# A GRU with a ternary FFN behind it: the FFN starts two groups behind the GRU, the first eight steps have two PSUM banks per sum, and the weight quantisation is spread over twelve steps

## The chip, the cores and the metric

One Trainium2 chip, one core of it. The metric is the device time of one execution in microseconds; lower is better. Before the change the median of 3 runs is 365.18 us (363.53 to 365.69).

## What is computed

A GRU runs over 32 time steps for 128 sequences of width 256, from a given first state. Every state then goes through an FFN whose weights are made ternary in groups of 64, and the result is added to the input. Biases of the GRU are not zero. All is float32 except the quantisation, which is bfloat16.

```python
def cell(h, x):
    gi = x @ W_ih + b_ih
    gh = h @ W_hh + b_hh
    r = sigmoid(i_r + h_r); z = sigmoid(i_z + h_z)
    n = tanh(i_n + r * h_n)
    h_new = (1.0 - z) * n + z * h

w = w_fp32.astype(bfloat16); w_g = w.reshape(-1, 64)
scale = clip(mean(abs(w_g)), 1e-08, None)
q = clip(round(w_g / scale), -1, 1)
w_hat = q * scale                      # used as w + (w_hat - w)

gu = x @ wq_gu.T                       # 256 -> 2 * 1024
h = silu(gate) * up
hn = h * rsqrt(mean(h * h) + eps)
return hn @ wq_p.T                     # 1024 -> 256
```

## The kernel before

One engine program each for SyncE (loads and stores), GpSimd (POOL), ScalarE (ACT), VectorE (DVE) and TensorE (PE), tied by semaphores. The order on every engine is written out by hand.

**The GRU step** (t = 0 to 31). Every float32 product is split in three passes of a rounded form: high parts of data and weights, high data by low weights, low data by high weights. PE's state product adds to the bank ps_rz (r and z, 512 columns, so one sigmoid serves both) and to the second half of ps_n (256 columns). ACT takes the sigmoid (L294). DVE makes r_hn and n_pre (L434, L436) and zh (L437), ACT the tanh (L307), DVE zm_n and the new state h_nat (L443, L446). PE transposes h_nat (L639), ACT rounds it to the high part (L311), DVE makes the low part (L450). With the high part the next state product can start. Between the sigmoid and the transposes PE adds the product of the next input to ps_rz, behind the transposes that to ps_n. Both banks are single: before the next input's product ACT copies the bias into them (seed_rz after the sigmoid, L299; seed_n after n_pre, L303). The split of the input is done by ACT (L314) and by DVE (L455), in steps 2 to 5 by GpSimd (L252).

**The FFN** works on groups of four steps, 512 columns, one group behind the GRU. Per group there are eight tiles j: gate product G and up product U (four matmuls of 512 columns each, L646), sigmoid on ACT (silu_part, L318), gated and hidden on DVE (L460, L470: gsg, then hid), hid_hi and the square on ACT (L322, L332), hid_lo and the sum of squares on GpSimd (L258, L265), and the down product D (eight matmuls of 256 columns, L685) into ps_out. C6 and C7 are the down products of tiles 6 and 7 of the group before, S its sums of squares by token. rows_out (L484) scales ps_out, adds the input from x_all and writes o_st, which SyncE stores. The items are placed among the steps by the tables PE_BEFORE and PE_AFTER (ahead of and behind the transposes; "in" and "n" are the next input's products). U of tile j waits for hid of tile j-1, since ps_up is one bank. A group's states must lie together, so at each fourth step ACT and DVE copy three states into grp_hi and grp_lo. After step 31 the last group runs alone by PE_ALONE.

**The quantisation** has six units of 1024 columns: four of the gate and up weights, two of the down weights. Per unit: Abs (L338) and Sign (L343) on ACT, group sums on PE (L724, two matmuls), means on ACT (L353), seven operations on DVE (two of scales L493, L494; ternary L502, L504; L509; L511; signed L516) and the rounded weight on ACT (L347). One unit is done per step, steps 0 to 5; in steps 4 and 5 beside the first FFN group. Raw weights lie in x_all, which is loaded with the input only when the last sign is done.

**Start.** Two bias rows come by DMA, three products with a row of ones spread them over the partitions (plain float32), four small matmuls follow (keep_clock), and the input product waits for the split of the input weights, the state product for that of the state weights. Groups 2 to 6 are in a hardware loop on each engine, groups 0, 1 and 7 are written out.

## Time and profile before

| what | value |
|---|---|
| median of 3 runs | 365.18 us (363.53 to 365.69) |
| profiled execution, its own time | 364.85 us |
| its span in the trace | 363.0 us |
| PE busy | 345.6 us, 95% of the span |
| DVE, ACT, POOL busy | 234.0 (64%), 225.6 (62%), 164.5 (45%) us |
| chain that ended last, PE's share | 81% |
| mean granted TensorE clock | 0.986 |
| load of x_all, 4 MB, from issue to landing | 13.5 us |

The span runs from the first to the last recorded instruction; the time is 1.85 us more. A page row gives an engine's busy time in tenths for 40 equal slices. PE is the matmul stream, PEld the weight loads beside it. A matmul's own duration has a tail that overlaps the next one, so on a full PE durations add up to more than the time. A timeline row has the start, the duration, engine, line, operation, output from input, shapes, count, and in brackets how long the engine sat idle before it and for whom.

### The profile page before, as it was taken

To read this page: it belongs to the slowest core of one execution; us is meant where nothing else is said; L and a number is where in the kernel's file an instruction comes from. 1 tells how busy PE (TensorE), PEld (TensorE's weight loads), DVE (VectorE), ACT (ScalarE), POOL (GpSimd) and SP (SyncE) were. 2 spreads that over 40 slices of the span, in tenths; PEclk is the share of its full clock that TensorE was granted. 3 is DMA by queue.
4 is the path that set the end of the run, shared out by engine and by line. 5 is a ranking of instruction groups with operands and counts; after the bars stand their busy time and mean duration, and the time that the engine had idled before them with its cause. 6 is when DMAs were issued, how large, how long until landed. Compare 5 with 4: busy or idle time off the path is not lost.

```text
span 363.0 us, 5759 instructions
## 1 busy us (share of the span) xinstructions
PE 345.6 (95%) x1959; PEld 296.8 (82%) x1962; DVE 234.0 (64%) x446; ACT 225.6 (62%) x422; POOL 164.5 (45%) x141
## 2 busy tenths in 40 slices
PE   6978888799999999999999999999999999999995
PEld 4756666688888898888888898888888898888884
DVE  3698998845865567555865567555865567456643
ACT  5898996557366566657366566657366566546650
POOL 1111014336455363446455363446455363448881
PEclk9989999899999999999999999999999999999997
DMA  7990019000000001000000001000000001000101
GB/s 238 378 397 0 2 47 413 4 2 0 28 32 0 3 1 58 0 0 0 31 27 0 0 0 58 0 0 0 32 26 0 0 0 60 0 1 2 58 2 58
DMA packets 5394, 17.75 MB, mean 49 GB/s; under 512 B 386, under 2 KB 2050, under 8 KB 4996
## 3 DMA queue, kind: packets, MB, share of 16 engines
q1 hardware_dynamic: 5380, 17.57, 12.5%
q8 instruction: 8, 0.13, 0.2%
q14 instruction: 6, 0.05, 0.0%
HBM read 13.38 MB, written 4.19 MB: 48 GB/s over the span
## 4 chain that ended last, share of the span: by engine, by line
PE 81%; DVE 9%; ACT 4%; issue 3%; DMA 1%; SPq 0%; POOL 0%; POOLq 0%; DVEq 0%
PE ps_out L685 16%; PE ps_gate L646 15%; PE ps_up L646 14%; PE ps_rz L627 4%; PE ps_rz L603 4%; PE ps_n L603 4%; PE ps_rz L628 4%; PE ps_rz L604 4%; PE ps_rz L631 4%; PE ps_n L604 3%; PE ps_n L606 3%; PE ps_rz L606 3%; PE ps_hT L639 2%; DVE o_st L509 2%; PE ps_gate L696 1%
## 5 line engine op out<-in xcount | busy, mean ns | idle before, releaser
L258 POOL TENSOR_TENSOR hid_lo<-work,hid_hi 128x512 fp32r<-128x512 f32 x63 | 82.3, 1307 | 145.5 <-ACT hid_hi L322 145.5
L460 DVE TENSOR_TENSOR work<-work,ps_gate 128x512 f32<-128x512 f32 x64 | 43.9, 685 | 44.2 <-ACT work L318 43.4
L265 POOL TENSOR_TENSOR sq_sum<-sq_sum,work 128x512 f32<-128x512 f32 x54 | 71.4, 1322 | 0.0
L646 PE MATMUL ps_gate<-grp_hi,wguT 128*128 128x512 f32 x128 | 50.9, 398 | 0.0
L646 PE MATMUL ps_up<-grp_hi,wguT 128*128 128x512 f32 x118 | 47.2, 400 | 3.3 <-DVE work L470 3.3
L646 PE MATMUL ps_gate<-grp_lo,wguT 128*128 128x512 f32 x128 | 50.3, 393 | 0.0
L294 ACT ACTIVATE rz<-ps_rz 128x512 f32<-128x512 f32 x32 | 19.0, 595 | 47.3 <-PE ps_rz L631 46.9
L322 ACT CAST hid_hi<-work 128x512 fp32r<-128x512 f32 x63 | 38.7, 615 | 14.2 <-DVE work L470 14.2
L646 PE MATMUL ps_up<-grp_lo,wguT 128*128 128x512 f32 x118 | 46.6, 395 | 0.0
L470 DVE TENSOR_TENSOR work<-work,ps_up 128x512 f32<-128x512 f32 x59 | 40.5, 687 | 8.3 <-PE ps_up L646 6.8
L318 ACT ACTIVATE work<-ps_gate 128x512 f32<-128x512 f32 x64 | 37.8, 590 | 11.3 <-PE ps_gate L646 11.2
L434 DVE TENSOR_TENSOR r_hn<-rz,ps_n 128x256 f32<-128x256 f32 x32 | 13.5, 420 | 48.4 <-PE ps_n L606 48.4
L685 PEld LDWEIGHTS ps_out<-wpT,hid_hi 128*128 128x128 f32 x256 | 38.1, 189 | 4.4 <-DVE o_st L484 0.5
L685 PE MATMUL ps_out<-wpT,hid_hi 128*128 128x256 f32 x256 | 41.2, 283 | 0.1
L685 PE MATMUL ps_out<-wpT,hid_lo 128*128 128x256 f32 x256 | 41.0, 282 | 0.0
L685 PEld LDWEIGHTS ps_out<-wpT,hid_lo 128*128 128x128 f32 x256 | 35.1, 189 | 0.0
L332 ACT ACTIVATE work<-work 128x512 f32<-128x512 f32 x55 | 34.6, 629 | 0.0
L646 PEld LDWEIGHTS ps_up<-grp_hi,wguT 128*128 128x128 f32 x118 | 22.2, 188 | 8.8 <-DVE work L470 4.5
L311 ACT CAST new_hi<-ps_hT 128x256 fp32r<-128x256 f32 x24 | 8.9, 373 | 30.4 <-PE ps_hT L639 30.3
L603 PE MATMUL ps_rz<-wi_hi,xT_hi 128*128 128x512 f32 x64 | 26.6, 416 | 1.1 <-ACT ps_rz L299 0.7
L646 PEld LDWEIGHTS ps_gate<-grp_hi,wguT 128*128 128x128 f32 x128 | 24.1, 188 | 3.6 <-issue 0.2
L646 PEld LDWEIGHTS ps_gate<-grp_lo,wguT 128*128 128x128 f32 x128 | 24.1, 188 | 3.3
(116 smaller groups left out, 713.3 us busy)
## 6 DMA issues: line engine op xcount, KB each, us to landing
x_all<-in_x_dram SPq DMA_DIRECT2D x1, 4096.0 KB, 13.5
out_dram<-o_st SPq DMA_DIRECT2D x7, 512.0 KB, 2.6
xT_all<-in_x_dram SPq DMA_DIRECT2D x1, 3072.0 KB, 19.5
x_all<-in_L_ffn_w_gate_up_dram SPq DMA_DIRECT2D x4, 512.0 KB, 9.3
x_all<-in_L_ffn_w_proj_dram SPq DMA_DIRECT2D x1, 1024.0 KB, 12.8
work<-in_L_cond_W_ih_dram SPq DMA_DIRECT2D x2, 384.0 KB, 4.0
work<-in_L_cond_W_hh_dram SPq DMA_DIRECT2D x2, 384.0 KB, 5.8
xT_all<-in_x_dram SPq DMA_DIRECT2D x1, 768.0 KB, 8.0
```

The costliest lines, as they stand in the source:

```text
L258: nc.gpsimd.tensor_tensor(hid_lo[:, j % RING], hid[:, j % 2], f32(hid_hi[:, j % RING]), ALU.subtract).then_inc(hid_lo_ok, 1)
L265: nc.gpsimd.tensor_tensor(sq_sum[:], sq_sum[:], hid_sq[:, j % 2], ALU.add).then_inc(sq_added, 1)
L318: nc.scalar.activation(sg[:, j % 2], ps_gate[:, j % 2], ACT.Sigmoid).then_inc(sg_ok, 1)
L322: nc.scalar.copy(hid_hi[:, j % RING], hid[:, j % 2]).then_inc(hid_hi_ok, 1)
L332: nc.scalar.activation(hid_sq[:, j % 2], hid[:, j % 2], ACT.Square).then_inc(hid_sq_ok, 1)
L460: nc.vector.tensor_tensor(gsg[:, j % 2], sg[:, j % 2], ps_gate[:, j % 2], ALU.mult).then_inc(gsg_ok, 1)
L470: nc.vector.tensor_tensor(hid[:, j % 2], gsg[:, j % 2], up_bank(G, j)[:], ALU.mult).then_inc(hid_ok, 1)
L603: pe.matmul(dst, hi[:, k, :], w_hi[:, k, cols], start=False, stop=False, skip_group_check=True)
L604: pe.matmul(dst, hi[:, k, :], w_lo[:, k, cols], start=False, stop=False, skip_group_check=True)
L606: mm = pe.matmul(dst, lo[:, k, :], w_hi[:, k, cols], start=False, stop=stop and k == KD - 1, skip_group_check=True)
L646: mm = pe.matmul(bank, w, part[:, k].rearrange("p s b -> p (s b)"), start=(k == 0 and i == 0), stop=(k == KD - 1 and i == 1))
L685: mm = pe.matmul(ps_out[:, s, :], part[:, j % RING, s * P:(s + 1) * P], wpT[:, j, :], start=(j == 0 and s % 2 == 0 and part is hid_hi), st ...
```

## The change

- The FFN starts behind step 7, not step 3. Steps 0 to 7 run alone, steps 8 to 31 carry groups 0 to 5 by the same tables (PE_FIRST takes the place of the last column for group 0, with D4 and D5 behind the transposes), and groups 6 and 7 run alone at the end, by PE_ALONE each (PE_END closes).
- In steps 0 to 7 each sum has two banks, ps_rz and ps_up, ps_n and a half of ps_gate, and PE itself adds the bias: the bias is split in a high and a low row with changed sign (b_split), multiplied by two rows of -1. ACT's bias copies start with step 8.
- The quantisation takes two steps per unit in steps 0 to 7 (units 0 to 3), and units 4 and 5 stand in pieces in steps 8 to 11. Units are in the order in which the FFN wants them, and the down weights load as two.
- States stay in rings of 12 (st_hi, st_lo); grp and its copies are gone. The input for the last addition lies in a ring of 24 rows, the last 8 are loaded after the second store.
- GpSimd splits the inputs of steps 2 to 9. PE begins with 12 and later 6 matmuls on zeros. No hardware loop is left, all groups are written out.

```diff
 QG = 64
 EPS = 2.0 ** -23
 RING = 4
+LEAD = 8
+SR = 12
+XR = 24
 
 
 PE_BEFORE = [["C6", "G0", "in", "C7", "S"], ["G2", "U2", "in", "D0"],
              ["G4", "U4", "in", "D2"], ["G6", "U6", "in", "G7", "D4", "U7"]]
 PE_AFTER = [["U0", "n", "G1", "U1"], ["n", "G3", "U3", "D1"], ["n", "G5", "U5", "D3"], ["n", "D5"]]
...
+PE_FIRST = [["G6", "U6", "in", "G7", "U7"], ["n", "D4", "D5"]]
...
+        def rz_bank(t):
+            return ps_up if early(t) and t % 2 else ps_rz
+
+        def n_bank(t):
+            return ps_gate[:, 0, :] if early(t) and t % 2 else ps_n[:]
+
...
-            free = isinstance(G, int) and (G == NG - 1 and j % 2 or G == NG - 2 and j == HT - 1)
+            free = G >= NG - 2 and j % 2 or G == NG - 3 and j == HT - 1
             return ps_rz if free else ps_up
...
+        def state(parts, t):
+            return parts[:, :, t % SR, :]
+
+        def group_state(parts, G, k):
+            first = GS * G % SR
+            return parts[:, k, first:first + GS, :].rearrange("p s b -> p (s b)")
+
+
+        units = [("gu", 0), ("gu", HT), ("pj", 0), ("gu", 4), ("gu", HT + 4), ("pj", 4)]
...
+            for u in range(1, NU):
+                load_unit(u)
+            sp.wait_ge(b_split_ok, 1)
+            sp.dma_start(xT_all[:, :, LEAD:T, :], xt[:, :, LEAD:T, :]).then_inc(ld_xr, 16)
             sp.wait_ge(q_sign_ok, NU)
-            sp.dma_start(x_all[:], x).then_inc(ld_x, 16)
...
+            sp.dma_start(x_ring[:], x[:, 0:XR, :]).then_inc(ld_x, 16)
...
+                if G == (T - XR) // GS - 1:
+                    sp.dma_start(x_ring[:, 0:T - XR, :], x[:, XR:T, :]).then_inc(ld_x, 16)
...
+            for t in range(2, LEAD + 2):
+                pool.wait_ge(x_hi, t + 1)
+                nc.gpsimd.tensor_tensor(xT_lo[:, t % 2], xT_all[:, :, t, :], f32(xT_hi[:, t % 2]),
                                         ALU.subtract).then_inc(x_lo_early, 1)
...
+            for t in range(LEAD):
+                u, odd = divmod(t, 2)
+                rz_gates(t)
+                if odd:
+                    q_signs(u)
+                elif u:
+                    q_means(u)
+                n_gate(t)
+                if odd:
+                    q_abs_of(u + 1)
+                elif u:
+                    q_weights(u - 1)
+                else:
+                    q_means(0)
+                state_hi(t)
+                if t == 0:
+                    act.wait_ge(ld_x1, 16)
+                if t == LEAD - 2:
+                    act.wait_ge(ld_xr, 16)
+                input_hi(t + 2)
...
+                if t == LEAD:
+                    q_means(4)
+                if t == LEAD + 1:
+                    q_means(5)
+                n_gate(t)
+                if t < T - 1:
+                    seed_n(t + 1)
+                if t == LEAD:
+                    q_weights(3)
+                if t == LEAD + 1:
+                    q_signs(4)
+                if s == 3:
+                    silu_part(G, 6)
+                if s:
+                    hidden_parts(G, 2 * s - 1)
+                silu_part(G, 7 if s == 3 else 2 * s)
+                state_hi(t)
+                if t == LEAD + 3:
+                    q_weights(5)
+                hidden_parts(G, 2 * s)
+                if s < 3:
+                    silu_part(G, 2 * s + 1)
+                if t == LEAD:
+                    q_abs_of(5)
+                if t == LEAD + 1:
+                    q_weights(4)
+                if t == LEAD + 2:
+                    q_signs(5)
...
+            nc.vector.memset(q_keep[:], 0.0).then_inc(warm_ok, 1)
...
+            nc.vector.tensor_tensor(b_all[:, RZ], b_all[:, RZ], b_rows[:, 0:2 * D], ALU.add).then_inc(b_sum_ok, 1)
+            dve.wait_ge(b_sum_ok, 1)
+            nc.vector.tensor_copy(b_hi, b_all).then_inc(b_hi_ok, 1)
...
+            nc.vector.scalar_tensor_tensor(out=b_split[:], in0=f32(b_hi), scalar=ident[0:2, 1:2], in1=b_all,
+                                           op0=ALU.mult, op1=ALU.subtract).then_inc(b_split_ok, 1)
...
+                u, odd = divmod(t, 2)
+                candidate(t)
+                new_state(t)
+                if odd:
+                    difference(u)
+                else:
+                    scales(u)
+                state_lo(t)
+                if odd:
+                    magnitude(u)
+                    signed(u)
+                else:
+                    ternary(u)
+
...
+                if t == LEAD + 1:
+                    difference(4)
+                    magnitude(4)
+                if t == LEAD + 2:
+                    ternary(5)
+                if t == LEAD + 3:
+                    magnitude(5)
+                    signed(5)
+                gated(G, 2 * s)
+                if s:
...
+                    ternary(4)
+                if t == LEAD + 1:
+                    signed(4)
+                    scales(5)
+                if t == LEAD + 2:
+                    difference(5)
+                if G and s == 0:
+                    rows_out(G - 1)
+
+            for G in (NG - 2, NG - 1):
...
+                return pe.matmul(dst, neg_ones[:], b_split[:, cols], start=start, stop=False, skip_group_check=True)
+
+            def seed_rz(t):
+                bias_rows(rz_bank(t)[:], RZ, True)
+
+            def seed_n(t):
+                bias_rows(n_bank(t)[:, 0:D], N_IN, True)
+                bias_rows(n_bank(t)[:, D:2 * D], N_HID, False)
+
+            def input_rz(t):
+                if t > LEAD:
+                    pe.wait_ge(rz_seed, t - LEAD)
+                if t < 2:
...
+                    pe.wait_ge(q_w_ok, 1 if j == 0 else 4)
+                if j == 1 and 0 < G < NG - 2:
...
+
+            pe.wait_ge(warm_ok, 1)
+            busy(12)
+            pe.wait_ge(consts, 5)
+            pe.wait_ge(b_split_ok, 1)
+            bias_rows(ps_gate[:, 1, :], RZ, True)
+            bias_rows(q_sums[:, 0, 0:D], N_IN, True)
+            bias_rows(q_sums[:, 0, D:2 * D], N_HID, False).then_inc(biased, 1)
+            seed_rz(0)
+            seed_n(0)
+            busy(6)
             pe.wait_ge(wi_ok, KD)
...
+                state_product(t)
+                seed_rz(t + 1)
+                input_rz(t + 1)
+                seed_n(t + 1)
+                if t == 0:
+                    pe.wait_ge(bias_ok, 2)
+                    q_group_sums(0)
+                transpose_state(t)
+                input_n(t + 1)
+                if t % 2:
+                    q_group_sums((t + 1) // 2)
+
+            for t in range(LEAD, T):
+                g, s = divmod(t, GS)
+                G = g - LEAD // GS
+                before, after = PE_BEFORE[s], PE_AFTER[s]
+                if s == 3 and G == 0:
+                    before, after = PE_FIRST
+                if s == 3 and g == NG - 1:
+                    before, after = PE_LAST
...
+                    q_group_sums(5)
 
...
+                ffn_item(NG - 2, item)
+            for item in PE_ALONE + PE_END:
+                ffn_item(NG - 1, item)
 
```

What moves on the engines shows in their instruction rows (line, operation, output from input, shape, count).

PE in step 1, from the last pass of the next input's product to the first matmul of the next state product. Before:

```order
L606 MATMUL ps_rz<-wi_hi,xT_lo 128x512 x2
L639 MATMUL ps_hT<-ident,h_nat 128x128 x2
L603 MATMUL ps_n<-wi_hi,xT_hi 128x256
L604 MATMUL ps_n<-wi_lo,xT_hi 128x256
L603 MATMUL ps_n<-wi_hi,xT_hi 128x256
L604 MATMUL ps_n<-wi_lo,xT_hi 128x256
L606 MATMUL ps_n<-wi_hi,xT_lo 128x256 x2
L627 MATMUL ps_rz<-wh_hi,new_hi 128x512
```

And after:

```order
L650 MATMUL ps_rz<-wi_hi,xT_lo 128x512 x2
L655 MATMUL ps_n<-b_split,neg_ones 128x256 x2
L698 MATMUL ps_hT<-ident,h_nat 128x128 x2
L645 MATMUL ps_n<-wi_hi,xT_hi 128x256
L646 MATMUL ps_n<-wi_lo,xT_hi 128x256
L645 MATMUL ps_n<-wi_hi,xT_hi 128x256
L646 MATMUL ps_n<-wi_lo,xT_hi 128x256
L650 MATMUL ps_n<-wi_hi,xT_lo 128x256 x2
L786 MATMUL ps_out<-q_abs,q_ones 128x512 x2
L645 MATMUL ps_rz<-wh_hi,st_hi 128x512
```

The bias rows L655 for the n bank now stand ahead of the transposes L698, and the group sums L786, which stood behind the state product (L724), now stand behind the input's n product and ahead of the next state product.

ACT in the first step that carries FFN work (step 4 before, step 8 after), from behind the split of the input to the end of the step; "work" holds sg, gsg, hid and its square. Before:

```order
L347 CAST wguT<-q_keep 128x2x512
L307 ACTIVATE n_act<-n_pre 128x256
L353 ACTIVATE q_mean<-ps_out 128x1024
L303 COPY ps_n<-bias 128x512
L318 ACTIVATE work<-ps_gate 128x512
L311 CAST new_hi<-ps_hT 128x2x128
L338 ACTIVATE q_abs<-x_all 128x1024
L322 CAST hid_hi<-work 128x512
L326 ACTIVATE sq_sum<-work 128x512
L318 ACTIVATE work<-ps_gate 128x512
L343 ACTIVATE q_sign<-x_all 128x1024
```

And after:

```order
L355 ACTIVATE q_mean<-ps_out 128x1024
L309 ACTIVATE n_act<-n_pre 128x256
L305 COPY ps_n<-bias 128x512
L349 CAST wguT<-q_keep 128x2x512
L320 ACTIVATE work<-ps_gate 128x512
L313 CAST st_hi<-ps_hT 128x2x128
L324 CAST hid_hi<-work 128x512
L328 ACTIVATE sq_sum<-work 128x512
L320 ACTIVATE work<-ps_gate 128x512
L340 ACTIVATE q_abs<-x_ring 128x1024
```

The means (L353, now L355) went ahead of the tanh (L307, now L309), the weight of the unit before behind it, and Abs (L338, now L340) from behind the state's copy to the very end, behind hid_hi, the square and the second sigmoid.

DVE in the last step of the first FFN group (step 7 before, step 11 after), from zm_n on. Before:

```order
L443 SCALAR_TENSOR_TENSOR zm_n<-rz,n_act 128x256
L446 TENSOR_TENSOR h_nat<-zh,zm_n 128x256
L455 TENSOR_TENSOR xT_lo<-xT_all,xT_hi 128x256
L460 TENSOR_TENSOR work<-work,ps_gate 128x512
L470 TENSOR_TENSOR work<-work,ps_up 128x512
L460 TENSOR_TENSOR work<-work,ps_gate 128x512
L470 TENSOR_TENSOR work<-work,ps_up 128x512
L450 TENSOR_TENSOR grp_lo<-ps_hT,grp_hi 128x2x128
L558 CAST grp_lo<-new_lo 128x2x384
```

And after:

```order
L459 SCALAR_TENSOR_TENSOR zm_n<-rz,n_act 128x256
L462 TENSOR_TENSOR h_nat<-zh,zm_n 128x256
L471 TENSOR_TENSOR xT_lo<-xT_all,xT_hi 128x256
L528 TENSOR_TENSOR o_st<-q_abs,o_st 128x1024
L533 TENSOR_TENSOR q_keep<-o_st,q_sign 128x1024
L476 TENSOR_TENSOR work<-work,ps_gate 128x512
L486 TENSOR_TENSOR work<-work,ps_up 128x512
L476 TENSOR_TENSOR work<-work,ps_gate 128x512
L486 TENSOR_TENSOR work<-work,ps_up 128x512
L466 TENSOR_TENSOR st_lo<-ps_hT,st_hi 128x2x128
```

The magnitude L528 and the signed value L533 of unit 5 now stand ahead of gated and hidden of tile 6 (L476, L486). In step 10 ternary(5), two operations, stands at the same place; before, steps 6 and 7 had no quantisation.

## Rows read from the trace of the kernel before

**Rows 1.** The page, busy tenths of PE in 40 equal slices:

```profile
PE   6978888799999999999999999999999999999995
```

**Rows 2.** Busy time by stretch (length, then each engine; clock; DMA share; GB/s):

```profile
core 0: us, PE busy (x) PEld busy (x) DVE busy (x) ACT busy (x) POOL busy (x), PEclk, DMA share, GB/s
43.10:52.70 9.60, 8.26 (x42) 6.45 (x41) 9.06 (x17) 8.60 (x15) 1.75 (x1) 1.00 0.00 0
52.71:65.04 12.33, 10.94 (x61) 8.89 (x61) 10.84 (x19) 7.85 (x14) 5.44 (x4) 1.00 0.84 342
65.05:78.83 13.78, 11.84 (x60) 9.84 (x59) 8.81 (x16) 7.06 (x13) 5.23 (x5) 0.88 0.00 0
78.84:88.84 10.00, 10.00 (x60) 8.75 (x59) 5.83 (x12) 7.69 (x15) 3.94 (x4) 1.00 0.01 2
88.85:129.63 40.78, 40.78 (x242) 35.91 (x241) 25.55 (x50) 24.81 (x51) 20.33 (x17) 1.00 0.04 14
330.22:353.85 23.63, 23.58 (x137) 20.53 (x137) 13.16 (x23) 13.60 (x25) 20.33 (x17) 1.00 0.06 24
353.85:363.00 9.15, 4.74 (x42) 4.54 (x40) 3.74 (x8) 0.62 (x1) 1.82 (x2) 0.80 0.15 57
```

**Rows 3.** Timeline, the sigmoid over r and z of steps 0 and 31:

```profile
13.71 0.60 ACT L294 ACTIVATE rz<-ps_rz 128x512 f32<-128x512 f32 x1
...
323.79 0.60 ACT L294 ACTIVATE rz<-ps_rz 128x512 f32<-128x512 f32 x1 [2.67 <-PE ps_rz L631]
```

**Rows 4.** Timeline of step 0, its chain and the group sums:

```profile
14.21 0.60 PE L724 MATMUL ps_out<-q_abs,q_ones 128*128 128x512 bf16 x2
...
15.42 0.42 ACT L307 ACTIVATE n_act<-n_pre 128x256 f32<-128x256 f32 x1
...
15.87 0.73 DVE L443 SCALAR_TENSOR_TENSOR zm_n<-rz,n_act 128x256 f32<-128x256 f32 x1
...
17.12 0.44 PE L639 MATMUL ps_hT<-ident,h_nat 128*128 128x128 f32 x2 [0.40 <-DVE h_nat L446]
...
18.11 0.41 PE L627 MATMUL ps_rz<-wh_hi,new_hi 128*128 128x512 f32 x1
...
19.78 0.59 ACT L294 ACTIVATE rz<-ps_rz 128x512 f32<-128x512 f32 x1
```

**Rows 5.** Timeline of the start, the last weight split and PE's products:

```profile
9.82 1.89 DVE L530 TENSOR_TENSOR wh_lo<-work,wh_hi 128x768 fp32r<-128x768 f32 x2 [0.31 <-ACT wh_hi L370]
9.85 0.63 PE L603 MATMUL ps_rz<-wi_hi,xT_hi 128*128 128x512 f32 x1
...
12.12 0.39 PE L627 MATMUL ps_rz<-wh_hi,grp_hi 128*128 128x512 f32 x1
```

**Rows 6.** Timeline of step 4 on ACT, first and last of four operations:

```profile
49.99 0.62 ACT L322 CAST hid_hi<-work 128x512 fp32r<-128x512 f32 x1 [0.46 <-DVE work L470]
...
51.52 1.05 ACT L343 ACTIVATE q_sign<-x_all 128x1024 bf16<-128x1024 f32 x1
```

**Rows 7.** Timeline of step 31, hid_hi on ACT and hid_lo on GpSimd:

```profile
326.27 0.61 ACT L322 CAST hid_hi<-work 128x512 fp32r<-128x512 f32 x1
...
326.96 1.30 POOL L258 TENSOR_TENSOR hid_lo<-work,hid_hi 128x512 fp32r<-128x512 f32 x1 [4.28 <-ACT hid_hi L322]
```

**Rows 8.** Step 5: a GpSimd operation, DVE's beside it; all six of one DVE line:

```profile
62.14 1.36 POOL L258 TENSOR_TENSOR hid_lo<-work,hid_hi 128x512 fp32r<-128x512 f32 x1 [0.58 <-ACT hid_hi L322]
...
62.37 1.67 DVE L504 TENSOR_TENSOR q_hat<-q_keep,q_scale 128x1024 bf16<-128x1024 bf16 x1
...
L509 DVE TENSOR_TENSOR o_st<-q_hat,q_abs x6: 691/694/1676, 19.8 to 64.1; 128x1024 bf16<-128x1024 bf16 x6
```

**Rows 9.** Transposes of steps 1 and 3, and a stretch behind the first:

```profile
24.30 0.44 PE L639 MATMUL ps_hT<-ident,h_nat 128*128 128x128 f32 x2 [1.60 <-DVE h_nat L446]
...
25.00:26.00 1.00, 1.00 (x6) 1.00 (x7) 0.85 (x3) 1.00 (x2) 0.00 (x0) 0.50 1.02 430
...
39.71 0.44 PE L639 MATMUL ps_hT<-ident,h_nat 128*128 128x128 f32 x2 [1.36 <-DVE h_nat L446]
```

## What the change will do to the time

> **What bounds the kernel now.** First the slices of the page: PE is at 9 from the ninth slice to the last but one, and lower only before that [rows 1]. So the time is PE's own work, except at the start. Then busy time by stretch, cut at the starts of the sigmoid over r and z (one per GRU step) [rows 2, 3]. From step 8 to step 12 PE is busy 40.78 of 40.78 us: four GRU steps and one FFN group, nothing to gain there. The losses stand ahead of it. Steps 0 to 3, which run without FFN, take 43.10 - 13.71 = 29.4 us, steps 4 to 7 (first FFN group) 9.60 + 12.33 + 13.78 + 10.00 = 45.7 us, where PE works 8.26 us in step 4 and a full step is 10.00, so some 38.3. The FFN group alone behind the GRU (from its first gate product to the point where the last one's closing items begin) takes 23.63 us with PE busy 23.58, and then 9.15 us follow. The whole sum to beat: step 12 begins at 129.63 and the rest takes 363.0 - 129.63 = 233.4 us.
>
> **What a step costs when nothing else is in it.** I follow the chain of step 0 [rows 4]: sigmoid at 13.71, tanh 1.71 later, the transposes 1.70 later (0.30 of it is a zm_n of 0.73 us where others take 0.43, so 1.40), the first state matmul 0.99 after the transposes, the next sigmoid 1.67 after that. 1.71 + 1.40 + 0.99 + 1.67 = **5.77 us**. Steps 1 to 3 took 43.10 - 19.78 = 23.3 us, 7.8 each: DVE ran five operations of 0.69 us of quantisation per step [rows 8], ACT four of about 1 us (a sign is 1.05 [rows 6]), and PE waited for ACT to write the bias into its one bank.
>
> **The change, part by part.**
> 1. *Start.* Bias products move and 18 warm-up matmuls come in, on a PE that waits anyway. The chain is ACT's and DVE's rounding of the weights: the last wh_lo ends at 9.82 + 1.89 = 11.71, and before, PE starts the state product only at 12.12, because it did the input products at the slow clock (a 512-column matmul is 0.63 us there and 0.39 later) [rows 5]. After: at 11.8. Gain 0.3, first sigmoid at 13.4. The DVE work for the bias (sum, split: three small operations) ends before wi_hi is there: nothing.
> 2. *Eight steps alone.* With two banks and PE bias rows, ACT's two bias copies and their waits are gone. The PE cost is one 512-column and two 256-column matmuls a step, 0.47 us, a little less than the 0.60 of the two L724 matmuls with their tail [rows 4]. They stand between sigmoid and transposes, 3.1 us in which PE else has 2.1 of work: nothing. DVE now has two or three quantisation operations a step: they end 5.8 us after the sigmoid at the plain durations, 6.5 with a hold by GpSimd, and the next r_hn is wanted at 6.5 (0.8 after the next sigmoid: tanh's 1.71 less two DVE operations of 0.45). ACT has two operations of about 1 us, which fit before tanh and before the state copy. Both just fit. On the path is one thing: after odd steps the group sums stand ahead of the state product, 0.47 us, four times, and in step 0 q_means waits for them and holds the state copy 0.3. So 4 x 5.77 + 4 x 6.24 + 0.3 = 48.3 us. Step 8's sigmoid is at 61.7.
> 3. *First FFN group, steps 8 to 11, with units 4 and 5.* PE's load: 8.26 (its sums are in that) + 3 x 10.0 = 38.3. Waits, each in us behind the step's sigmoid. **Step 8**: q_means stands ahead of tanh and delays it 0.7; hid of tile 0 is ready at 6.4; ACT then does hid_hi, square, sigmoid (from 49.99 to 51.52 in the old group, 1.53 [rows 6]) and only then Abs of unit 5 (1.06): 9.1. PE has been free since 7.4 and its next items are the sums of unit 5, then the state product: 9.1 + 0.5 + 1.6 = 11.2. **Step 9**: sign of unit 4 on ACT and two operations on DVE delay hid of tile 2, U3 waits 0.7: 10.8. **Step 10**: the two operations of ternary(5) come on DVE at 3.3, GpSimd's hid_lo at 3.2 (hid_hi begins 2.5 and hid_lo 3.2 behind the sigmoid [rows 7]). Two such operations then took 1.67 us each and not 0.69 [rows 8]. Hid of tile 4 comes at 8.1 where PE wants it at 6.5: 11.6. **Step 11**: magnitude and signed stand ahead of gated(6), one is held 1.0: 1.45 + 1.0 more, hid of tile 6 at 7.1. PE_FIRST puts U7 right behind G7, at 4.6: wait 2.5. After it the transposes, the state copy and only then q_weights(5) (1.05) on ACT, for which D4 waits 0.9: 13.4. Sum 11.2 + 10.8 + 11.6 + 13.4 = **47.0 us**; its floor is 38.3 plus step 8's 1.7 wait and its tanh delay, some 40.5; its ceiling is 47 + twice 1.7 (below) = 50.4. I take 47.0, as the old group with the same two units took 45.7 and collided in the same way.
> 4. *Steps 12 to 31* keep their item tables: the same 40.8 us for four. The copies of grp_hi and grp_lo, gone with the ring, lay on ACT and DVE under PE's work: nothing.
> 5. *Two groups alone instead of one.* The extra one costs what the table PE_ALONE costs now, **23.6 us** [rows 2]. GpSimd is busy 20.33 of it and DVE 13.16, so it can be repeated without another bound.
> 6. *Loads.* x_ring is sent for once sign(5) is done, in step 10 at about 94 us; it is 3 MB where 4 MB took 13.5 us (table above), and wanted by rows_out(0) at about 113. Nothing.
>
> Sum of the span: 13.4 + 48.3 + 47.0 = 108.7 for the start of step 12 (before 129.6: 20.9 earlier), + 233.4 + 23.6 = **365.7 us**. The profiled execution before had a span of 363.0 and a time of 364.85, 1.85 more, which I add: 367.5. Its 364.85 lies inside the runs (363.53 to 365.69, median 365.18), so against the median it is 0.6% more. In short: step 12 begins 20.9 us earlier, but the FFN work taken from beside four GRU steps costs nearly as much alone, because PE was already full beside them.
>
> *A rule beside the trace.* Rows 8 show DVE and GpSimd alternating: 1.67 us for operations that take 0.69 when GpSimd is still. The Trainium skill (SBUF — State Buffer, Who interferes with whom, and the section on the two sides) says that the pair of ports is an exclusive lock, taken by VectorE operations in a two-port mode or with two SBUF inputs against a GpSimd one; the trace agrees. By the rule the two scalings of unit 5 in step 9 would be held too, which no row here shows; with one hold of 1.0 more the sum would be 366.7.
>
> **The rivals.**
> *A. The quantisation hides (the other side).* The place is DVE in steps 10 and 11: if GpSimd's operations fall a few tenths later than I reckon, no hold occurs, tile 4 and tile 6 come 1.0 to 2.0 earlier, and the group takes 40.5 to 43. For it: in steps 0 to 4 the same operations ran in full next to ACT with no hold. Against: where GpSimd's FFN work and such an operation met, the operation was held [rows 8]. Time with the group at its floor: 13.4 + 48.3 + 40.5 + 257.0 = 359.2, + 1.85 = 361.0. It decides at a group of 41 us: below that the kernel is faster by over 1%.
> *B. PE's clock falls.* After a wait of 1.60 us for h_nat, PE ran at half clock, 1.2 GHz (granted 0.50); after one of 1.36 it did not [rows 9]. The fall in step 6 gives the price: a mean of 0.88 over 13.78 us is 3.3 us at half clock, 1.7 us of work lost [rows 2]. I count waits of 1.7 (step 8, some work within), 1.6 (step 10) and 2.5 us (step 11) in the new group. One fall costs up to 1.7, two 3.4, less where PE would wait anyway. Time 367.5 + 1.0 to 3.4 = 368.5 to 370.9. For it: the waits are as long as the one that did it. Against: step 11's slow stretch lies partly over the wait for q_weights(5).
> *C. The eight steps don't become short.* If DVE's last quantisation operation misses r_hn by 0.4 in each step, 3 us more: 370.5. Against it the sum in part 2, with nothing to spare, though.
>
> **How the numbers follow.** A measurement of this kernel can tell about 1% from no change, 361.5 to 368.8. The sum as it stands, with its small errors: 0.43. A: 0.27, at 361.0. B and C together: 0.30, at 370. The time is the sum's, 367.5. The likeliest case's own range is 364 to 369; for 8 in 10 I reach from 360.0, within A, to 371.0, the end of B. Faster 0.27, same 0.43, slower 0.30.
>
> **What would show it.** Sigmoid of step 8 at 61.7 (range 60 to 65) and of step 12 at 108.7 (102 to 112). Spacings alternate 5.8 and 6.2 in the steps alone. In steps 8 to 11 PE waits: before the L786 sums for ACT's q_abs, before U3, U5 and U7 for DVE's hid, before D4 for wpT; DVE operations of 1.7 us beside GpSimd's; a granted clock under 1.00 means B. Four steps from 12 on take 40.8, and two groups of 23.6 us stand at the end. It would be wrong if PE waits in the unrolled part for its own instructions, or if two groups alone in a row do not keep 23.6 us each, or if the group with units 4 and 5 is under 41 us.

## The result, and the profile after

The changed kernel takes **369.72 us** (median of 4 runs, 369.60 to 370.07) where the kernel before takes 365.18 (363.53 to 365.69): the ratio is 1.0134, with a 95% interval of 1.0101 to 1.0167. So it is slower by 1.3%. The predicted 367.5 was 2.2 us too low; the range of 360.0 to 371.0 holds the time; and the case that came was the one given a chance of 0.30, not the likeliest one. The profiled execution took 370.07 us with a span of 368.3, 5.3 more than the 363.0 before.

The page of the changed kernel, PE and its granted clock in the 40 slices:

```profile
span 368.3 us, 5360 instructions
...
PE   7999999798969999999999999999999999999995
...
PEclk9999999999899999999999999999999999999997
```

Against [rows 1] the first slices are fuller, yet the span is longer. PE's share of busy time rose and so did the time, so that share alone does not tell whether a change helped. Next is busy time by stretch, cut at the sigmoids of steps 0, 8, 9, 10, 11, 12 and 16, then the two FFN groups at the end and what follows them (columns as in [rows 2]):

```profile
13.90:62.02 48.12, 47.31 (x240) 35.74 (x243) 38.15 (x76) 27.58 (x47) 9.63 (x8) 1.00 0.28 109
62.02:73.12 11.10, 8.94 (x46) 6.80 (x45) 7.34 (x16) 7.55 (x13) 1.72 (x1) 1.00 0.00 0
73.12:83.99 10.87, 10.28 (x60) 8.73 (x59) 8.67 (x14) 8.59 (x16) 5.82 (x4) 1.00 0.01 2
83.99:98.00 14.01, 12.03 (x60) 9.97 (x59) 10.82 (x17) 6.94 (x14) 5.60 (x5) 0.88 0.12 30
98.00:111.48 13.48, 10.56 (x60) 8.76 (x59) 7.53 (x13) 8.00 (x16) 6.16 (x5) 1.00 0.48 204
111.48:152.26 40.78, 40.78 (x242) 35.93 (x241) 23.74 (x49) 24.17 (x48) 19.16 (x16) 1.00 0.03 14
312.04:335.70 23.66, 23.61 (x138) 20.55 (x138) 12.73 (x22) 13.31 (x24) 20.02 (x17) 1.00 0.06 23
335.70:359.30 23.60, 23.55 (x140) 20.56 (x138) 12.60 (x22) 13.30 (x24) 20.06 (x17) 1.00 0.06 23
359.30:368.30 9.00, 4.83 (x38) 4.53 (x37) 3.40 (x8) 0.62 (x1) 1.48 (x2) 0.71 0.16 60
```

Step 12 starts at 111.48, 18.1 us earlier than the 129.63 of before, and the rest takes 368.3 - 111.48 = 256.8 where it took 233.4. The difference, 23.4, is the second FFN group that now runs alone, so what the later start of the FFN gains is more than handed back at the end. Where the prediction had hoped for more is the first FFN group, steps 8 to 11: 11.10 + 10.87 + 14.01 + 13.48 = 49.46 us, with PE at work for 41.81 of them. Here are PE's waits in that group from 0.5 us up, from the timeline:

```profile
65.78 0.44 PE L698 MATMUL ps_hT<-ident,h_nat 128*128 128x128 f32 x2 [0.79 <-DVE h_nat L462]
...
71.08 0.60 PE L786 MATMUL ps_out<-q_abs,q_ones 128*128 128x512 bf16 x2 [1.36 <-ACT q_abs L340]
...
80.40 0.50 PE L705 MATMUL ps_up<-st_hi,wguT 128*128 128x512 f32 x1 [0.59 <-DVE work L486]
...
92.87 0.51 PE L705 MATMUL ps_up<-st_hi,wguT 128*128 128x512 f32 x1 [1.79 <-DVE work L486]
...
105.03 0.51 PE L705 MATMUL ps_up<-st_hi,wguT 128*128 128x512 f32 x1 [2.23 <-DVE work L486]
...
107.86 0.75 PE L745 MATMUL ps_out<-wpT,hid_hi 128*128 128x256 f32 x4 [0.69 <-ACT wpT L349]
```

These are the transposes of step 8, for a state that the means ahead of tanh made late, the sums of unit 5, then U3, U5 and U7 for DVE's hid, then D4 for the last weights: the places and, within 0.4 us, the lengths that the prediction named. Behind the wait of 1.79 us the clock fell (stretches of 1 us, same columns):

```profile
93.00:94.00 1.00, 1.00 (x4) 0.80 (x5) 0.75 (x2) 1.00 (x3) 0.45 (x1) 0.71 0.00 0
94.00:95.00 1.00, 1.00 (x6) 0.91 (x5) 0.48 (x1) 1.00 (x3) 1.00 (x2) 0.50 0.00 0
95.00:96.00 1.00, 1.00 (x6) 1.00 (x6) 0.90 (x2) 0.43 (x1) 1.00 (x1) 0.50 0.00 0
```

A granted clock of 0.50 is 1.2 GHz, half the speed. And why hid of tile 4 was late stands on GpSimd and DVE (timeline, steps 9 and 10):

```profile
81.08 1.49 POOL L265 TENSOR_TENSOR hid_lo<-work,hid_hi 128x512 fp32r<-128x512 f32 x1 [0.20 <-ACT hid_hi L324]
81.34 1.51 DVE L510 TENSOR_SCALAR q_half<-q_mean 128x1024 bf16<-128x1024 bf16 x1
82.53 1.47 POOL L272 TENSOR_TENSOR sq_sum<-sq_sum,work 128x512 f32<-128x512 f32 x1
82.78 1.51 DVE L511 TENSOR_SCALAR q_scale<-q_mean 128x1024 bf16<-128x1024 bf16 x1
...
87.96 1.30 POOL L265 TENSOR_TENSOR hid_lo<-work,hid_hi 128x512 fp32r<-128x512 f32 x1 [3.96 <-ACT hid_hi L324]
88.01 1.79 DVE L518 TENSOR_TENSOR q_keep<-q_half,q_abs 128x1024 bf16<-128x1024 bf16 x1
89.21 1.74 POOL L272 TENSOR_TENSOR sq_sum<-sq_sum,work 128x512 f32<-128x512 f32 x1
89.84 1.66 DVE L520 TENSOR_TENSOR q_hat<-q_keep,q_scale 128x1024 bf16<-128x1024 bf16 x1
```

Four DVE operations, each beside a GpSimd one and each 1.0 to 1.1 us over its plain 0.42 or 0.69, as in [rows 8]. Such an operation is called held below.

### The profile page after: what moved, and what is told of

It reads as the page before. It is cut to its first block, busy times and chain, and to the rows that moved or that the text cites. A ratio compares the mean times of both kernels' runs of the same rounds, so it can differ in the third digit from the quotient of the medians.

```text
span 368.3 us, 5360 instructions
## 1 busy us (share of the span) xinstructions
PE 352.6 (96%) x1992; PEld 298.7 (81%) x1996; DVE 229.5 (62%) x438; ACT 211.5 (57%) x398; POOL 170.8 (46%) x144
## 4 chain that ended last, share of the span: by engine, by line
PE 85%; DVE 5%; ACT 5%; issue 2%; DMA 1%; POOL 0%; SPq 0%; DVEq 0%
PE ps_out L745 16%; PE ps_gate L705 14%; PE ps_up L705 13%; PE ps_rz L645 7%; PE ps_rz L646 6%; PE ps_rz L650 6%; PE ps_n L645 3%; PE ps_n L646 3%; PE ps_n L650 3%; PE ps_rz L705 2%; PE ps_hT L698 2%; DMA work<-in_L_cond_W_ih_dram 1%; PE ps_up L645 1%; PE ps_gate L758 1%; PE ps_up L646 1%
## 5 line engine op out<-in xcount | busy, mean ns | idle before, releaser
L476 DVE TENSOR_TENSOR work<-work,ps_gate 128x512 f32<-128x512 f32 x64 | 43.9, 685 | 45.2 <-ACT work L320 44.4
L705 PE MATMUL ps_gate<-st_hi,wguT 128*128 128x512 f32 x128 | 50.6, 395 | 0.0
L705 PE MATMUL ps_gate<-st_lo,wguT 128*128 128x512 f32 x128 | 50.3, 393 | 0.0
L705 PE MATMUL ps_up<-st_hi,wguT 128*128 128x512 f32 x110 | 44.2, 402 | 4.8 <-DVE work L486 4.8
L324 ACT CAST hid_hi<-work 128x512 fp32r<-128x512 f32 x63 | 38.8, 615 | 16.8 <-DVE work L486 16.8
L450 DVE TENSOR_TENSOR r_hn<-rz,ps_n 128x256 f32<-128x256 f32 x28 | 11.8, 422 | 51.7 <-PE ps_n L650 51.7
L705 PE MATMUL ps_up<-st_lo,wguT 128*128 128x512 f32 x110 | 43.5, 395 | 0.0
L486 DVE TENSOR_TENSOR work<-work,ps_up 128x512 f32<-128x512 f32 x55 | 37.8, 687 | 8.6 <-PE ps_up L705 6.4
L313 ACT CAST st_hi<-ps_hT 128x256 fp32r<-128x256 f32 x32 | 11.9, 372 | 36.8 <-PE ps_hT L698 36.8
L259 POOL TENSOR_TENSOR xT_lo<-xT_all,xT_hi 128x256 fp32r<-128x256 f32 x8 | 9.6, 1204 | 49.9 <-ACT xT_hi L316 49.9
L705 PEld LDWEIGHTS ps_up<-st_hi,wguT 128*128 128x128 f32 x110 | 20.7, 188 | 10.5 <-DVE work L486 5.9
L705 PEld LDWEIGHTS ps_gate<-st_lo,wguT 128*128 128x128 f32 x128 | 24.1, 189 | 3.3
L705 PEld LDWEIGHTS ps_gate<-st_hi,wguT 128*128 128x128 f32 x128 | 24.1, 188 | 3.2
```

What stands on the lines that cost most here:

```text
L324: nc.scalar.copy(hid_hi[:, j % RING], hid[:, j % 2]).then_inc(hid_hi_ok, 1)
L476: nc.vector.tensor_tensor(gsg[:, j % 2], sg[:, j % 2], ps_gate[:, j % 2], ALU.mult).then_inc(gsg_ok, 1)
L486: nc.vector.tensor_tensor(hid[:, j % 2], gsg[:, j % 2], up_bank(G, j)[:], ALU.mult).then_inc(hid_ok, 1)
L705: mm = pe.matmul(bank, w, group_state(part, G, k), start=(k == 0 and i == 0), stop=(k == KD - 1 and i == 1))
```

## The experiments

The lead is the number of steps that run before the first FFN group: 8 in the change, 4 before. All spans below are of one profiled execution; the changed kernel's is 368.3, the kernel before's 363.0. Ratios are to the kernel before on the same chip, with the 95% interval. My theory had two parts: (1) steps 8 to 11 are long because the quantisation of units 4 and 5 stands, partly held by GpSimd, ahead of what PE waits for; (2) a second group of lead costs by itself, since a step alone takes 5.7 us and more. The rivals are: VectorE has no room for the work in any order, or the steps alone are where the loss is.

### Is it GpSimd that holds DVE?

```diff
+                w_lo = slice(0, 16) if G == 0 and j >= 4 else slice(0, 512)
+                w_sq = slice(0, 16) if G == 0 else slice(0, 512)
```
(the columns of GpSimd's subtraction and of its sum)

> Of the changed kernel, GpSimd's sum of squares for the first FFN group works on 16 of the 512 columns, and hid_lo of that group's tiles 4 to 7 too, so the first group's output is not the reference's (its sums of squares and the low halves of four tiles are mostly left out); nothing is moved. Theory (VectorE's bfloat16 operations on unit 5 are held while GpSimd is in its 512-column operations, and what they make late is what TensorE waits for in steps 10 and 11): the second scaling of unit 5 in step 9 (1.51 us now) and the ternary operation that lies beside the sum of squares in step 10 (1.66) come back to about .42 and .7, U5 of step 10 waits under 0.7 us in place of 1.79, TensorE's clock does not fall behind it, U7 of step 11 waits about 1 in place of 2.23; the way from step 8's sigmoid to step 12's falls from 49.5 to 44.5 to 46.5, the span by 3 to 5 us, with steps 0 to 7 and 12 to 31 as they are. Rival (the operations are slow of themselves or VectorE simply has too much to do there): those operations keep 1.5 us, U5 waits over 1.2 us and the span moves by under 1 us.

Span 363.6, ratio 1.0038 (1.0016 to 1.0059). Timeline of DVE and, last, PE:

```profile
80.91 1.52 DVE L512 TENSOR_SCALAR q_half<-q_mean 128x1024 bf16<-128x1024 bf16 x1
82.35 0.44 DVE L513 TENSOR_SCALAR q_scale<-q_mean 128x1024 bf16<-128x1024 bf16 x1
...
88.79 0.69 DVE L522 TENSOR_TENSOR q_hat<-q_keep,q_scale 128x1024 bf16<-128x1024 bf16 x1
...
90.86 0.50 PE L707 MATMUL ps_up<-st_hi,wguT 128*128 128x512 f32 x1 [0.50 <-DVE work L488]
```

The scaling beside the full-width hid_lo keeps 1.52 us, and so does the comparison (q_keep) with its 1.79; the scaling beside the shortened sum falls from 1.51 to 0.44, q_hat from 1.66 to 0.69. The same instructions, in the same order, are fast when GpSimd's neighbour is short: the hold is GpSimd's. Steps 8 to 11 take 45.20 us in place of 49.46, as the theory said. U5 waits 0.50, U7 1.27 in place of 2.23, the clock stays at 1.00, and steps 10 and 11 take 10.74 and 12.49 us in place of 14.01 and 13.48:

```profile
83.70:94.44 10.74, 10.24 (x60) 8.69 (x59) 8.76 (x15) 6.94 (x13) 2.44 (x4) 1.00 0.04 9
94.44:106.93 12.49, 10.52 (x60) 8.73 (x59) 6.56 (x13) 7.99 (x15) 1.77 (x6) 1.00 0.62 246
```

That also prices step 10: the same items are 10.24 us of PE at full clock and were 12.03, so the fall cost 1.79 us, and the waits 1.98 - 0.50 = 1.48 more.

### Is it the place of the quantisation?

```diff
-PE_FIRST = [["G6", "U6", "in", "G7", "U7"], ["n", "D4", "D5"]]
+PE_FIRST = [["G6", "U6", "in", "G7", "U7"], ["n"]]
+PE_SECOND = ["G0", "in", "B4", "B5", "C6", "C7", "S"]
...
-                if t == LEAD:
-                    scales(4)
...
                 state_lo(t)
...
+                if t == LEAD + 3:
+                    difference(5)
+                    magnitude(5)
+                    signed(5)
```
(PE_SECOND is step 12's list; B4 and B5 are D4 and D5 of group 0. Not shown: the other operations of units 4 and 5 on DVE, and ScalarE's part, where the means stand behind tanh, Abs of unit 5 ahead of the hidden parts of step 8, and the last weights in step 12)

> All arithmetic is kept. Units 4 and 5 are quantised in steps 8 to 11 as now, but each VectorE operation stands behind state_lo of its step and not ahead of the step's gated tiles, ScalarE's means stand behind tanh, Abs of unit 5 is done in step 8 ahead of the hidden parts, the last weights (projection rows of tiles 4 to 7) are copied in step 12, and the down products D4 and D5 of the first group move to step 12 beside C6 and C7. Theory (what costs time in steps 8 to 11 is the place of the quantisation in the in-order queues of VectorE and ScalarE, ahead of what TensorE waits for): the four steps fall from 49.5 to 41 to 45 us, step 12 grows from 10.9 to about 12.4 with two more down products, and the span falls by 4 to 7 us; TensorE's clock stays at 1.00. Rival (it is the amount of work on VectorE in these steps that is too much, wherever it stands): the hidden operations come late all the same, U3, U5 and U7 still wait 4 us together and the span moves by under 1.5 us.

Span 364.9, ratio 1.0056 (1.0032 to 1.0080). Steps 8 to 11 fell from 49.46 to 39.88 us, more than hoped for (2.2 us of it are D4 and D5, which went to step 12), but step 12 took 17.65, the clock fell in it, and the span fell by 3.4 us only, under the 4 to 7 of the theory. The timeline of DVE and PE around it:

```profile
100.24 1.68 DVE L524 TENSOR_TENSOR o_st<-q_hat,q_abs 128x1024 bf16<-128x1024 bf16 x1
101.96 1.66 DVE L528 TENSOR_TENSOR o_st<-q_abs,o_st 128x1024 bf16<-128x1024 bf16 x1
103.65 1.66 DVE L533 TENSOR_TENSOR q_keep<-o_st,q_sign 128x1024 bf16<-128x1024 bf16 x1
...
107.53 0.74 PE L742 MATMUL ps_out<-wpT,hid_hi 128*128 128x256 f32 x4 [3.14 <-ACT wpT L350]
```

Three held products in a row made step 12's candidate, its tanh and the copy of the last weights late; PE waited 3.14 us and the clock fell. The next kernel spreads them: one product in each of steps 9 to 11 ahead of the step's gated tile, where DVE waited for ScalarE, and one behind state_lo in step 11.

```diff
+                if t == LEAD + 1:
+                    difference(4)
+                if t == LEAD + 2:
+                    keep_above(5)
+                if t == LEAD + 3:
+                    magnitude(5)
                 gated(G, 2 * s)
```
(keep_above is the comparison, the first half of ternary)

> All arithmetic kept, FFN two groups behind. As the run with the quantisation later, but no step of the four holds more than three of the products of unit 4 or 5: one product stands ahead of the step's gated tile, where VectorE waited 1.7 us for ScalarE (difference of 4 in step 9, the comparison of 5 in step 10, magnitude of 5 in step 11), the scalings of 5 move to step 9 and difference of 5 to step 10, so that step 11 has one product behind state_lo in place of three. Theory (in that run three held products of 1.66 us at the end of step 11 made step 12's candidate late, D4 waited 3.14 us and the clock fell behind that): steps 8 to 11 stay at 39.5 to 41.5 us, D4 of step 12 waits under 1.2 us, the clock stays at 1.00, step 12 falls from 17.65 to 12.5 to 14, the span from 364.9 to 360 to 362. Rival (VectorE has no room for the held products in these four steps in any order): the waits come back in steps 9 to 11 and the span stays within 1.5 us of 364.9.

Span 360.6, ratio 0.9946 (0.9928 to 0.9963), as expected. Steps 8 to 11, then step 12:

```profile
61.97:101.74 39.77, 38.18 (x206) 31.16 (x205) 33.94 (x59) 30.21 (x55) 17.14 (x12) 1.00 0.21 80
101.74:114.76 13.02, 13.00 (x82) 11.16 (x81) 9.03 (x16) 5.87 (x12) 6.74 (x6) 1.00 0.06 24
```

Steps 8 to 12 take 52.8 us where the changed kernel takes 60.3, with the same operations, five of the fourteen still held (1.51 to 1.78 us). VectorE had room; what was lacking was the right order, and not VectorE's alone. From sigmoid to sigmoid steps 8 to 11 now take 8.90, 10.50, 11.22 and 9.15 us where they took 11.10, 10.87, 14.01 and 13.48. The first 2.2 us are ScalarE's: with Abs of unit 5 and the means moved, PE no longer waits in step 8 (0.79 and 1.36 us before). Of the last 4.3 us, 2.2 are D4 and D5, which step 12 pays. No run moved the two engines' operations one without the other, so the whole 7.5 us is shown for both together.

### What does the second group of lead cost?

```diff
-                nc.scalar.copy(unit_part(u, wguT, wpT), q_keep[:]).then_inc(q_w_ok, 1)
+                nc.scalar.copy(unit_part(u, wguT, wpT), unit_part(u, wgu, wpj)).then_inc(q_w_ok, 1)
```
(and every other operation of the quantisation left out; the second kernel also has LEAD = 4)

> The changed kernel without the quantisation: ScalarE copies the weights as they are loaded (one copy for each of the six units, a unit a step), so the FFN's weights are not ternary and the output is not the reference's. FFN two groups behind, as in the change. It is to be read beside the same with a lead of four steps. Theory (a step alone is bound by its chain of latencies, so it costs 5.6 us for 4.4 us of TensorE's own work, while with an FFN group beside it TensorE is full): eight steps alone 44 to 46 us, first FFN group 40.5 to 41.5, span 355 to 358, and 4.5 to 6 us longer than the one with a lead of four. Rival (the second group of lead costs nothing, since its FFN group runs alone at TensorE's full rate at the end, and only the quantisation's place was bad): the two differ by under 1.5 us.

> The same without the quantisation (raw weights copied, output not the reference's), and with the FFN one group behind the GRU, as in the kernel before: four steps alone instead of eight, one FFN group alone at the end instead of two; two banks and TensorE's bias in the four steps alone. Theory: four steps alone 22 to 23.5 us, each four steps with an FFN group 40.8, span 350 to 353; it is shorter than with a lead of eight by 4 times 5.6 plus 23.6 less 40.8, some 5.2 us. Rival: within 1.5 us of the one with a lead of eight.

Spans 355.0 and 349.4, ratios 0.9778 (0.9739 to 0.9818) and 0.9641 (0.9598 to 0.9683). The difference of the spans is 5.6 us, and the sum holds: step 8's sigmoid of the one less step 4's of the other is 59.69 - 36.66 = 23.03 us for four more steps alone, plus 23.6 for the group alone at the end, less 40.8: 5.8. The medians, 356.57 and 351.40, are 5.2 apart, since with a lead of four a time is some 2.2 us over its span and not 1.8. The first FFN group takes 38.6 and 38.8 us in them, 2 us less than expected, and the span with a lead of four is 0.6 under the range given for it. So a second group of lead is a loss of 5.2 to 5.6 us that only the quantisation's room can pay for.

With all arithmetic, a lead of four and the spread order, one whole unit has to fit in each step alone:

```diff
-LEAD = 8
+LEAD = 4
...
-                if t % 2:
-                    q_group_sums((t + 1) // 2)
+                q_group_sums(t + 1)
```

> All arithmetic kept. The change without its two groups of lead: the FFN begins one group behind the GRU, as before; the four steps alone have two banks and TensorE's bias and quantise one whole unit each (units 0 to 3), and units 4 and 5 are quantised in steps 4 to 7 by the spread order. Theory (the second group of lead is what costs, the banks and the later quantisation are what gain): the four steps alone take 26 to 29 us (29.4 before), steps 4 to 7 39.5 to 42 (45.7 before), step 8 two us over its usual 10.9; the span comes to 355 to 359, 4 to 8 us under the kernel before. Rival (eight steps were needed to hide the quantisation): the four steps alone take over 31 us, or D4 and G4 wait for late weights over 3 us together, and the span is at 361 or more, no better than before.

Span 368.8, ratio 1.0165 (1.0124 to 1.0206): the numbers are the rival's, but not for its reason. Steps 0 to 3 took 38.6 us, and the cause was this kernel's order on PE:

```profile
20.88 0.95 PE L788 MATMUL ps_out<-q_abs,q_ones 128*128 128x512 bf16 x2 [2.66 <-ACT q_abs L343]
```

The next unit's group sums stood ahead of the state product on PE, and Abs was not ready. The next kernel puts a unit's sums one step later, behind that step's own state product (and reorders ScalarE's items in these steps).

```diff
                 state_product(t)
+                q_group_sums(t)
...
-                q_group_sums(t + 1)
+                if t == LEAD - 1:
+                    q_group_sums(LEAD)
```

> All arithmetic kept. As the run with a lead of four and two banks, whose steps alone took 9.4 us since TensorE, in order, stood at the group sums of the next unit (up to 2.7 us, for Abs) ahead of the next state product. Here a step's group sums stand behind its own state product, one step after Abs, and ScalarE copies the last unit's weights between sigmoid and tanh and makes the means behind tanh. Theory (that wait alone made it slow): the steps alone take 7.0 to 7.4 us each (27.5 to 29.5 together, 29.4 before), steps 4 to 7 stay at 39.8, and the span is 368.8 less 9 to 10.5, 358 to 360, 3 to 5 us under the kernel before. Rival (VectorE's whole unit in each step alone is too much by itself): over 8 us a step, span 362 or more.

Span 361.8, ratio 0.9978 (0.9957 to 1.0000). That is between the two: steps 0 to 3 take 31.8 us, not the 27.5 to 29.5 of the theory, and the middle two 7.60 each, with DVE busy for 6.9 of them. In step 3 PE waited 1.43 us for the new state and, after 1.15 us of work, once more, and the clock fell: 10.18 us.

```profile
40.73 1.06 ACT L343 ACTIVATE q_abs<-x_ring 128x1024 bf16<-128x1024 f32 x1
...
42.25 0.63 PE L789 MATMUL ps_out<-q_abs,q_ones 128*128 128x512 bf16 x1 [1.42 <-POOL xT_lo L262]
```

Only one of the two matmuls of these sums is on record, and Abs, for which they wait in the program, ended at 41.79; so the second wait was rather 1.0 us than the 1.42 of the row, and for Abs. Moving those last sums too:

> All arithmetic kept, FFN one group behind. The last run with a lead of four, with one thing moved: the group sums of unit 4 stand behind step 4's state product and not ahead of it, where TensorE waited 1.42 us for Abs and ran at half clock afterwards (10.18 us from step 3's sigmoid to step 4's). Theory: that step comes to 7.5 to 7.7 us, like the two ahead of it, the clock does not fall, step 4 grows by up to .5, and the span falls from 361.8 to 359 to 360, 3 to 4 us under the kernel before. Rival (the clock falls there anyway, behind the 1.43 us wait for the new state ahead of the transposes): 8.5 us or more for that step and a span above 360.5. Beside the run with a lead of eight this also says what the second group of lead costs with the same quantisation: without any quantisation it was 5.6 us, here units 0 to 3 have to fit in four steps, 7.6 us each by VectorE's full queue, so the difference should be 0 to 1 us.

Span 360.8, ratio 0.9950 (0.9929 to 0.9970): nearer to the rival, whose span of over 360.5 it is, though the step took 8.32 us and not 8.5. The wait for Abs is gone, and the clock fell nevertheless (a stretch of 1 us in step 3):

```profile
42.00:43.00 1.00, 1.00 (x3) 0.79 (x3) 0.96 (x2) 1.00 (x2) 0.99 (x1) 0.50 0.00 0
```

### What is a step alone bound by?

```diff
-                input_rz(t + 1)
-                seed_n(t + 1)
...
+                seed_rz(t + 1)
...
-            return ps_up if early(t) and t % 2 else ps_rz
+            return ps_rz
```
(undone for the eight steps: one bank each, ScalarE seeds them)

> One part is undone: in the eight steps alone the sums lie in ps_rz and ps_n again, one bank each, and ScalarE's copies of the bias seed them, as in the kernel before; r and z stay in one product and the quantisation stays spread. Theory (the second bank takes the bias copy and the input product off the way from one sigmoid to the next): each of the eight steps gets 0.3 to 0.6 us longer, step 8's sigmoid comes 2.5 to 4.5 us later and the span grows by as much. Rival (TensorE was waiting for the state anyway, so the banks gave nothing, and the gain of the steps alone came from the spread quantisation): under 1 us in all.

Span 370.6, ratio 1.0186 (1.0147 to 1.0225). Even and odd steps take 6.05 and 6.52 us in place of 5.67 and 6.10; the eight take 50.69 in place of 48.12, 2.6 us more. The run also gives the bias back to ScalarE, but the next run shows that with two banks this changes nothing, so the 2.6 us are the second banks'. PE's waits (us in all, times, longest):

```profile
PE ps_rz L647 <- ACT ps_rz L301: 4.9, 8, 0.6
...
PE ps_hT L700 <- DVE h_nat L464: 4.6, 8, 0.8
```

Next the banks stay and ScalarE seeds them, two steps ahead:

```diff
                 input_hi(t + 2)
+                if t < LEAD - 1:
+                    nc.scalar.copy(rz_bank(t + 2)[:], bias[:, 0, :]).then_inc(rz_seed, 1)
+                    nc.scalar.copy(n_bank(t + 2), bias[:, 1, :]).then_inc(n_seed, 1)
```

> One part is undone: in steps 0 to 7 of the changed kernel the two banks stay, but from step 2 on ScalarE's copies of the bias seed them (two steps ahead, behind the split of the input), and TensorE's two bias seeds, .43 and .46 us of every step, are gone. Theory A (a step alone is bound by TensorE, which stands without a gap in steps 2 to 7): the even steps fall from 5.67 to about 5.2 or below and the odd ones from 6.10 to about 5.5, the span by 3 to 5 us. Theory B (the way from sigmoid over tanh, new state, transposes and state product is 5.67 us by itself and TensorE's order only fills it, but the odd steps' group sums, .43, are now hidden): even steps stay at 5.6 to 5.7, odd ones fall to about 5.7, the span by 1.2 to 1.8 us. Theory C (ScalarE's copies come in the way of the state's high part): no gain or up to 2 us more.

Span 367.8, ratio 1.0157 (1.0115 to 1.0199); the eight steps take 48.12 us, to the hundredth what they took. Even steps are theory B's, 5.67, but the odd ones stay at 6.10 where B had 5.7; the sum is what C said, not for C's reason. Its timeline in an even step, where the changed kernel shows the transposes without a wait:

```profile
39.57 0.62 PE L653 MATMUL ps_up<-wi_hi,xT_lo 128*128 128x512 f32 x2
41.23 0.44 PE L701 MATMUL ps_hT<-ident,h_nat 128*128 128x128 f32 x2 [1.03 <-DVE h_nat L465]
```

PE's 0.9 us of bias (start to start) turned into 1.03 us of waiting. PE looks full in the changed kernel's steps alone (47.31 of 48.12), but the chain from sigmoid to sigmoid is what takes 5.67 us. The next run changes the order of the odd steps alone, in the changed kernel:

```diff
                 if odd:
-                    q_signs(u)
+                    q_abs_of(u + 1)
...
+                if t % 2:
+                    q_group_sums((t + 1) // 2)
                 transpose_state(t)
                 input_n(t + 1)
-                if t % 2:
-                    q_group_sums((t + 1) // 2)
```

> Only the order inside the eight steps alone is changed: in an odd step ScalarE does Abs of the next unit ahead of tanh and Sign behind it, and TensorE does the group sums of the next unit ahead of the state's transposes. Theory (an odd step takes 6.10 us and an even one 5.67 because of what stands around tanh and the transposes in it): the odd steps come to 5.6 to 5.8, the even ones stay at 5.67, the first stays at 6.7; step 8's sigmoid starts 1.2 to 1.8 us earlier and the span falls by as much. Rival (the odd step is longer because of its banks, ps_up and ps_gate): the odd steps stay at 6.1 and the span moves by under 0.4 us. A second rival: the group sums, 0.8 us of TensorE, make the transposes late, and odd steps grow to 6.4 or more, the span by 1 us or more.

Span 366.8, ratio 1.0131 (1.0089 to 1.0173). Odd steps take 6.02 us, a gain of 0.3 us over the eight: neither theory. (The rest of the span's 1.5 us is a start that was 0.4 earlier and a first group that was 0.8 shorter.) With the bias on PE there is no gap ahead of the transposes, so the sums delay them instead of the state product. Only both together leave the sums in the gap:

> All arithmetic kept, FFN two groups behind; the run with the quantisation spread, and in the steps alone ScalarE's seeds (two banks) together with the other order of the odd steps: Abs ahead of tanh, the group sums ahead of the transposes. Theory (with TensorE's bias seeds gone it waits 1.0 us for the new state ahead of every transpose; the group sums, .43 us, cost the odd steps .43 only because they stand outside that wait, and inside it they are free): even steps 5.65 to 5.70, odd steps 5.65 to 5.75 in place of 6.10, steps 8 to 12 as in the run with the quantisation spread (52.8 together), the span 1.5 to 2 us under its 360.6. Rival (Abs ahead of tanh makes tanh late, or Sign behind it the state's high part): odd steps stay at 6.0 or above and the span within 0.6 us of 360.6.

Span 359.0, ratio 0.9906 (0.9881 to 0.9932), as expected: every step alone from the second on takes 5.66 to 5.68 us, and this is the best of the kernels that do all the arithmetic, 0.9% under the kernel before. Its steps 0 to 7, 8 to 11, and 12:

```profile
13.99:60.39 46.40, 40.57 (x223) 31.38 (x222) 37.74 (x76) 34.66 (x61) 9.65 (x8) 1.00 0.29 112
60.39:100.15 39.76, 38.16 (x206) 31.15 (x205) 34.35 (x59) 30.19 (x56) 17.15 (x12) 1.00 0.20 80
100.15:113.17 13.02, 13.00 (x82) 11.16 (x81) 9.01 (x16) 5.87 (x12) 6.74 (x6) 1.00 0.06 26
```

## Why the prediction was right or wrong, point by point

- *What bounds the kernel.* Right: steps 12 to 15 take 40.78 us before and after, with PE busy in all of it.
- *Part 1, the start: 13.4.* Measured 13.90, nothing gained (13.71 before). The second half of wi_hi waited 1.35 us for its DMA where it had waited 0.77, so the last wh_lo ended at 12.15 and not at 11.71, and the state product started at 12.20 for the 11.8 said. The slow clock of this part was read from durations of 0.63 us; the view of that stretch prints a granted clock of 1.00, so no row says it. In the twelve kernels of the experiments, whose start is all but the same, the first sigmoid is at 13.41 to 14.20; so 13.4 was the lower end and not the middle of it.
- *Part 2, eight steps alone: 48.3.* Measured 48.12; even 5.67 (5.77 said), odd 6.10 (6.24 said), step 0 6.73 (6.07 said). That the sum came out is in part luck: step 0 was 0.7 longer, since the means held the state copy 1.1 us and not 0.3, and the seven others together 0.9 shorter. Rival C is out. The bias costs PE 0.43 + 0.46 us a step and not the 0.47 in all that I reckoned (in step 4 it starts at 39.08, and the input product behind it at 39.51), but the cover I named, PE's gap ahead of the transposes, hid it: shown by ScalarE's seeds, which changed nothing. That the sums cost each odd step 0.43 (0.47 said) is shown by the last version, where they are free.
- *Part 3, first FFN group: 47.0.* Measured 49.46. Step 8 11.10 (11.2), step 9 10.87 (10.8), step 11 13.48 (13.4): right in time and in the waits that make them. **Step 10 is the one that failed**: 14.01 for 11.6. Its wait was 1.79 + 0.19 for 1.6, and its PE work 10.24 for 10.0; the remaining 1.8 us are the clock's fall, which I had put into rival B. The mechanism and the price (1.7, measured 1.79) stood in the prediction, but the sum put this term at nothing, although it named waits as long as the one that had brought the fall before [rows 9].
- *Part 4 and 5.* Right: the rest of the GRU and two groups of 23.66 and 23.60 took 256.8 us, 257.0 said. *Part 6*, the loads: nothing waited for x_ring.
- *The rule beside the trace.* By the Trainium skill (SBUF — State Buffer, Who interferes with whom) the scalings of unit 5 can be held too, and they were: 1.51 us each. The trace agrees, and so does the light-GpSimd run, in which one of the two became 0.44. That its 366.7 lies a little nearer to the span of 368.3 is luck for the larger part: step 9 took 10.87 us for the 10.8 said, and in step 10 the waits, which these holds can have lengthened, are 0.4 over; the rest is the clock.
- *Rival A, the quantisation hides.* Not in this order. The spread order comes near its floor of 40.5: it takes 39.8 us for the four steps and 2.2 in step 12 for D4 and D5, 42.0 in all.
- *Rival B.* It came, in step 10 and not in step 11. With one fall, 367.5 + 1.8 = 369.3, beside 370.07 for the profiled execution; what remains is the start (0.5) and tenths.

In sum the change took an FFN group out of four steps, which got 17.8 us shorter by it (40.8 to 23.0), and ran it alone in 23.6: 5.8 us lost. It bought room for the quantisation, and shorter steps alone. The arithmetic with both: eight steps, the first group and one group alone take 46.4 + 39.8 + 23.6 = 109.8 us in the best version with a lead of eight, and 30.0 + 40.4 + 40.8 = 111.2 with a lead of four (steps 0 to 3, 4 to 7, and a full group of four steps; the 2.2 us of D4 and D5 come on top in both). So with the quantisation inside, the two leads are within 1.5 us of each other in the best versions found. The one with a lead of four still has a fall of the clock in it, behind which step 3 took 8.32 us and not 7.60, so which lead is the better one is not shown. What made this change slower than the kernel before is the order within steps 8 to 11 (both engines'), some 7.5 us, and the sums in the odd steps, 1.7: without these two losses, and with ScalarE's seeds, it is 0.9% faster.

Left open: the run without quantisation and a lead of eight has one step alone of 6.10 us among those of 5.67, with no sums in it. In that step r_hn starts 1.19 us behind the sigmoid and in the others 0.77, while PE's n sum stands at its usual place; what held DVE there is not shown.

## What to carry to other kernels

Before work is taken from beside a chain and put alone at the end, price it: the steps that lose their companion get no shorter than their chain (5.67 us here), and the work taken out costs its full time. If DVE's extra operations are spread, put one where DVE waits for another engine and the rest behind the last operation that TensorE needs in that step; three held ones in a row ahead of the next step's first cost a wait of 3.14 us here. An engine that reads 98% busy can still have its time to spare: take some of its work away and see whether the step shortens or a wait appears.

## What the runs showed of the hardware

- The length of a wait does not decide alone whether TensorE's clock falls. In the changed kernel it fell to 0.50 behind U5's 1.79 us and not behind U7's 2.23; in the run with the order of the odd steps changed, the same waits were 1.76 and 2.24 us, and the clock fell behind the second only (step 11 took 14.29, step 10 12.46). In the first kernel with a lead of four it fell behind a wait of 1.96 us in step 1 and not behind another of 1.96 in step 3. In the last kernel with that lead it fell behind the third of three waits of 1.43 us, 7.6 us apart, and not behind the first two. Behind the seven waits of 1.02 to 1.03 us with ScalarE's seeds it did not fall. A fall cost 1.79 us of PE's time in the changed kernel, 1.5 in the run with the quantisation later (14.51 us of work in step 12, and 13.00 for the same items in the next), 1.4 in that with the odd steps' order (11.92 and 10.56).
- A DVE operation in bfloat16 of one input (0.42 us) is held as a two-input one (0.69) is: 1.51 and 1.66 to 1.79 us beside a GpSimd operation of 1.3 to 1.7. Held operations are not lost time as such: the spread order still has five of them.
- A bias product with two rows costs PE 0.43 us for 512 columns, where a full product behind another takes 0.23 (start to start). The products beside it start farther apart too: in step 4 the input product's last pass starts 1.78 us behind the state's last one with the bias between them (38.76 to 40.54) and 1.15 without (38.42 to 39.57, ScalarE's seeds), 0.63 us in all.
